# A ring of ten quarters for gathered rows, and VectorE's work placed anew between the links of a chain, in a graph-attention layer

## The chip, the cores and the metric

The kernel runs on one core of one Trainium2 chip. The metric is the device time of one execution in microseconds (us), the median of three timed runs. A further execution was taken with the hardware profiler; its rows are what is read here.

## The reference

One layer of a graph transformer over 3125 nodes of 256 channels, with 50,000 edges sorted by target node. Normalised rows give q, k and v; every edge has a score for each of 8 heads; a softmax over the edges of one target weighs the v rows. A linear attention over all nodes and a mixture of 8 experts stand beside and behind it.

```python
xn = _layernorm(x, axis=-1)
q = xn @ Wq.T + bq; k = xn @ Wk.T + bk; v = xn @ Wv.T + bv
sim = einsum('hed,hed->eh', q[:, dst], k[:, src]) * scale
m = segment_max(sim, dst); p = exp(sim - m[dst]); s = segment_sum(p, dst)
agg = segment_sum((p / s[dst]) * v[src], dst)
x = x + agg @ Wo.T + bo + linear_attention(xn)
x = x + experts(_layernorm(x))
```

## The kernel before

The program runs in stages, each a block of its own that all engines enter together: projections and edge tables (to about 150 us), linear attention (to 204 us), the graph attention (204 to 908.5 us), `finish` (output projection, second norm, routing, to about 970 us) and the experts.

**The graph attention** goes over the edges in 28 chunks (`CH`) of 16 steps of 128 edges; the last chunk has 8 steps. A step is one gather: an indirect DMA that GpSimd issues and that brings 128 rows of k and v (520 floats each, `KV`) from DRAM. Four steps are a quarter (`q` in the code). For chunk n the engines do this:

- GpSimd: per step one index copy and one gather (`gather`, L965, copy L955). Chunk c lies in `slot0` or `slot1` by its parity, four quarters each. Ahead of quarter q of chunk c GpSimd waits until VectorE's `weigh` of the same quarter of chunk c - 2 is done (`pv_made`, `QUADS * c + u // 4 + 1 - 2 * QUADS`).
- TensorE: `spread_q` (L1197) copies the q rows of the targets to the edges; `sums` (L1207) adds the weighted v rows by target, in two pairs of steps per quarter.
- VectorE: `product` (L1058) and `reduce` (L1065) make the scores of a quarter; `weigh` (L1074) multiplies the gathered v by the weights; `add` (L1088) adds a pair's sum to `agg`; `turned_hots` (L1052) makes the table of one-hots for the next `spread_q`.
- ScalarE: `hots` (L992, L996) makes the one-hots for `sums`, here through a buffer `habs`.

**The chain.** The running maxima of a chunk c go through links on several engines: `turn_scores` (TensorE, L1214), `local_maxima` (VectorE, L1100 and L1102), `ends` (TensorE, L1218, L1219), the copy to `row` (ScalarE, L1027), `carries` (VectorE, L1106 to L1111), `columns` (TensorE L1224, then VectorE L1115), `maxima` (VectorE, L1119 to L1123), the exponential (ScalarE, L1035), `turn_weights` (TensorE, L1230), and then `weigh(c, 0)`.

**What sets the order.** Each engine's order is written out by hand in a `body(n, ...)`, called for n = 0 to 29. In round n VectorE makes the scores of chunk n, runs the chain of chunk c = n - 1 and weighs and adds the rest of chunk b = n - 2. Engines run their own order and meet at semaphores. A round is named here by its `local_maxima`. Twelve passes of a hardware loop of two rounds each cover chunks 2 to 25.

`weigh` of (c, 0) and (c, 1) stands late in round c + 1, `weigh` of (c, 2) at the start of round c + 2, and `weigh` of (c, 3) behind that round's `carries`. `m.base` (125 x 25 x 256, the residual) is touched again only in `finish`, and `woT` too.

## Time and profile before

| | us |
|---|---|
| median of 3 timed runs | 1229.21 |
| lowest and highest | 1227.22, 1231.34 |
| the profiled execution | 1221.9 |
| its span (first to last instruction) | 1220.2 |
| graph attention within it | 204 to 908.5 |

The profiled execution is 7.3 us shorter than the median of the timed ones. Of the graph attention, 25 rounds from the second `local_maxima` at 246.95 us to the twenty-seventh at 875.87 us are alike and take 628.92 us, 25.16 us each. Rounds are read here by the wait that an engine ends last on, not by the share of busy time.

### The profile page before, as it was taken

To read this page: it belongs to the slowest core of one execution; us is meant where nothing else is said; L and a number is where in the kernel's file an instruction comes from. 1 tells how busy PE (TensorE), PEld (TensorE's weight loads), DVE (VectorE), ACT (ScalarE), POOL (GpSimd) and SP (SyncE) were. 2 spreads that over 40 slices of the span, in tenths; PEclk is the share of its full clock that TensorE was granted. 3 is DMA by queue.
4 is the path that set the end of the run, shared out by engine and by line. 5 is a ranking of instruction groups with operands and counts; after the bars stand their busy time and mean duration, and the time that the engine had idled before them with its cause. 6 is when DMAs were issued, how large, how long until landed. Compare 5 with 4: busy or idle time off the path is not lost. (4 is left out here: it accounts for less than half of the span.)

```text
span 1220.2 us, 18503 instructions
## 1 busy us (share of the span) xinstructions
PE 940.9 (77%) x4059; PEld 648.3 (53%) x4060; DVE 867.9 (71%) x1761; ACT 478.9 (39%) x1312; POOL 681.8 (56%) x1043
## 2 busy tenths in 40 slices
PE   4899776676777677787777768776768389999996
PEld 3455453454545455555555545554546246666664
DVE  3778767778888788887888788887968604444333
ACT  3556535434444344533444334443433033222330
POOL 2534276567778777787778877887500212222321
PEclk9999877878889877887788878888889779999998
DMA  4344272366566655566556655555413143233310
GB/s 146 103 103 95 79 225 77 89 175 191 164 175 184 179 166 164 170 175 179 153 169 163 173 153 163 154 158 161 116 46 109 63 142 124 90 111 102 137 59 8
DMA packets 79290, 164.39 MB, mean 135 GB/s; under 512 B 15472, under 2 KB 46963, under 8 KB 79251
## 3 DMA queue, kind: packets, MB, share of 16 engines
q0 software_dynamic: 38464, 110.26, 32.7%
q1 hardware_dynamic: 38883, 52.22, 13.3%
q10 hardware_dynamic: 1904, 1.45, 0.4%
q8 instruction: 16, 0.26, 0.1%
q14 instruction: 23, 0.19, 0.1%
HBM read 162.03 MB, written 17.65 MB: 147 GB/s over the span
## 5 line engine op out<-in xcount | busy, mean ns | idle before, releaser
L965 POOL DMA_INDIRECT slot<-kv_d,idx x408 | 426.6, 1046 | 149.3 <-DVE at_pv L1074 87.5
L1207 PE MATMUL at_pa<-at_pv,at_hot 128*125 128x264 f32 x880 | 288.5, 472 | 135.4 <-DVE agg L1088 133.3
L1207 PEld LDWEIGHTS at_pa<-at_pv,at_hot 128*125 128x125 f32 x880 | 186.7, 229 | 214.1 <-DVE agg L1088 140.2
L1197 PE MATMUL at_pq<-q,at_hotT 125*128 x1320 | 190.0, 306 | 11.1 <-POOL at_sign L951 7.0
L1058 DVE TENSOR_TENSOR at_prod<-at_pq,slot 128x1024 f32<-128x1024 f32 x110 | 134.0, 1218 | 76.6 <-DMA slot<-kv_d,idx 72.0
L1197 PEld LDWEIGHTS at_pq<-q,at_hotT 125*128 125x128 bf16 x1320 | 138.8, 109 | 46.0 <-issue 13.9
L1074 DVE TENSOR_TENSOR at_pv<-slot,at_pp 128x1056 f32<-128x1056 f32 x110 | 136.9, 1244 | 15.0 <-PE at_pp L1230 14.8
L992 ACT ACTIVATE at_habs<-iota_w,nloc_e 128x125 f32<-128x125 f32 x440 | 138.0, 384 | 3.4
L1065 DVE TENSOR_REDUCE at_sc<-at_prod 128x32 f32<-128x1024 f32 x110 | 133.4, 1213 | 2.0
L996 ACT ACTIVATE at_hot<-at_habs,one_col 128x500 f32<-128x500 f32 x110 | 78.3, 712 | 126.0 <-PE at_pa L1207 122.6
L1613 POOL DMA_INDIRECT out<-slot,node_s x32 | 31.9, 997 | 166.9 <-DVE slot L1645 166.0
L1680 PE MATMUL xp<-slot,hm 128*128 128x256 f32 (+1 forms) x512 | 113.1, 379 | 0.0
L1634 DVE TENSOR_TENSOR y<-xp,b 128x256 f32<-128x256 f32 (+1 forms) x32 | 13.6, 424 | 139.3 <-PE xp L1680 139.3
L1670 PE MATMUL xp<-hT,slot 128*128 128x489 f32 x256 | 108.6, 583 | 0.8 <-ACT hT L1578 0.8
L1680 PEld LDWEIGHTS xp<-slot,hm 128*128 128x128 f32 (+1 forms) x512 | 94.3, 185 | 18.2 <-issue 3.5
L1088 DVE TENSOR_TENSOR agg<-agg,at_pa 125x264 f32 x220 | 92.6, 421 | 7.6 <-PE at_pa L1207 2.8
L1027 ACT ACTIVATE at_row<-at_pchain 1x256 f32<-1x256 f32 x28 | 10.5, 376 | 202.9 <-PE at_pchain L1219 202.9
L1589 ACT ACTIVATE hm<-xp,b 128x489 f32<-128x489 f32 x64 | 42.9, 671 | 114.5 <-PE xp L1670 114.5
L955 POOL COPY idx<-src_e 128x1 int32 (+1 forms) x408 | 80.5, 198 | 2.6
L1670 PEld LDWEIGHTS xp<-hT,slot 128*128 128x128 f32 x256 | 49.5, 194 | 55.7 <-issue 49.9
L1224 PE MATMUL at_pchain<-at_one_c,at_line 1*128 1x1 f32 x112 | 25.0, 323 | 45.5 <-DVE at_line L1109 45.5
L629 PE MATMUL pa<-slot,xnT 128*125 128x512 f32 x100 | 51.7, 642 | 4.1 <-DVE vst L436 4.1
(316 smaller groups left out, 1263.7 us busy)
## 6 DMA issues: line engine op xcount, KB each, us to landing
slot<-in_w SPq DMA_DIRECT2D x16, 1024.0 KB, 6.3
locrow<-loc_d SPq DMA_DIRECT2D x28, 500.0 KB
slot<-kv_d,idx POOLq DMA_INDIRECT x408, 3.8
kv_d<-vst SPq DMA_DIRECT2D x25, 128.9 KB
base<-in_x SPq DMA_DIRECT2D x5, 625.0 KB
kv_d<-kst SPq DMA_DIRECT2D x25, 125.0 KB
row_d<-base SPq DMA_DIRECT2D x5, 625.0 KB
out<-base SPq DMA_DIRECT2D x1, 3125.0 KB
```

Source lines behind the costliest of these rows:

```text
L955: pool.tensor_copy(m.idx[:, par, u:u + 1], at(m.src_e, c)[:, u:u + 1]).then_inc(S.idx_ready, 1)
L965: pool.indirect_dma_start(slot[par][:, u, :], None, m.kv_d, bass.IndirectOffsetOnAxis(ap=m.idx[:, par, u:u + 1].bitcast(U32), axis=0), bou ...
L992: last = act.activation(habs[:, u % 4, :], m.iota_w[:, :], ACT.Abs, bias=at(m.nloc_e, c)[:, u:u + 1])
L996: act.activation(hot[:, 4 * (g % 2):4 * (g % 2) + 4, :], habs[:, :, :], ACT.Relu, bias=m.one_col[:, 0:1], scale=-1.0).then_inc(S.hot_made, 1)
L1058: dve.tensor_tensor(prod[:, q % 2, :, :], pq[q % 2].rearrange("p (i d) -> p i d", i=4), slot[par][:, 4 * q:4 * q + 4, 0:D], ALU.mult).then ...
L1065: dve.tensor_reduce(sc[:, :, 4 * q:4 * q + 4].rearrange("p h i -> p i h"), prod[:, q % 2, :, :].rearrange("p i (h d) -> p i h d", h=H), X, ...
L1074: dve.tensor_tensor(pv[:, 4 * (q % 2):4 * (q % 2) + 4, :, :], slot[par][:, four, D:KV].rearrange("p i (h c) -> p i h c", h=H), spread(ph[: ...
L1088: dve.tensor_tensor(dst, dst, pa[p % 2][:, 0:H * VW].rearrange("p (h c) -> p h c", h=H), ALU.add).then_inc(S.added, 1)
L1197: mm = pe.matmul(pq[q % 2][:, u * D:(u + 1) * D], hotT[:, 4 * q + u, :], at(m.q3, wins[u // 2])[:, part, :], start=(part == 0), stop=(part ...
L1207: mm = pe.matmul(pa[p % 2][:, 0:H * VW], hot[:, u % 8, :], pv[:, u % 8, :, :].rearrange("p h c -> p (h c)"), start=(u % 2 == 0), stop=(u % ...
L1670: mm = pe.matmul(p1[f % 2][:, 0:CAP], w1[par][:, c, f * 128:(f + 1) * 128], hT[par][:, c, 0:CAP], start=(c == 0), stop=(c == 1))
L1680: mm = pe.matmul(p2[i % 2][0:sizes[i], 0:D], hm[:, f, 128 * i:128 * i + sizes[i]], w2[par][:, f, :], start=(f == 0), stop=(f == FC - 1))
```

## The change

- **Ring.** Gathered rows lie in ten quarters instead of two slots of four: the eight of `slot0` and `slot1`, and two more. Number eight lies where the first 8 tiles (`SOON`) of `m.base` are (with 32 floats more per partition), number nine in a new `m.extra` that also holds `woT`. GpSimd waits ahead of a quarter for the `weigh` of the quarter ten back.
- **Spill.** At the start of the graph attention SyncE stores those 8 tiles (1000 KB) and `woT` (264 KB) to DRAM, ahead of its first load of `locrow`; behind the last `weigh` it loads both back. GpSimd's first two quarters of chunk 2 wait for the store. TensorE's first output projection in `finish`, and VectorE's first addition to `base`, wait for the load.
- **Room.** `prod` has one buffer instead of two; `habs` is gone: `hots` writes `hot` directly, and waits for `summed` ahead of its first instruction; some small tiles of other stages move into `extra`.
- **Loop.** Four passes of five rounds, with three rounds ahead and seven behind, in place of twelve passes of two.
- **Order.** VectorE: `weigh(b, 3)` and `add(b, 2, 0)` stand ahead of `carries`; `product` and `reduce` of quarter 1 stand between `carries` and `columns`; `product` and `reduce` of quarter 2 and `turned_hots` stand between `maxima` and `weigh(c, 0)`. TensorE: `turn_scores` stands ahead of `spread_q(n, 1)`, `ends` ahead of `sums(b, 2)`, `spread_q(n, 2)` ahead of `columns`, `spread_q(n, 3)` ahead of `turn_weights`, and `spread_q(n + 1, 0)` ahead of `sums(c, 0)`.

VectorE in a round near the end, before, from the first scan of the chain to `weigh(c, 0)` (the rows between `fall` and the maxima are `weigh(b, 3)` and the adds of quarter 2):

```order
L1065 TENSOR_REDUCE at_sc<-at_prod 128x4x8 [waits sc_turned,prod_made]
L1106 SCALAR_TENSOR_TENSOR at_run<-at_stop,at_row 1x144 [waits chain_act]
L1107 SCALAR_TENSOR_TENSOR at_run<-at_stop,at_row 1x144
L1109 COPY at_line<-at_run 1x256 [waits chain]
L1110 COPY at_row<-at_run 1x8
L1111 TENSOR_TENSOR at_fall<-at_run 1x8
L1074 TENSOR_TENSOR at_pv<-slot,at_pp 128x1056 [waits summed]
L931 TENSOR_LOAD win_of
L1088 ISA [waits added,summed]
L1088 TENSOR_TENSOR agg<-agg,at_pa 125x264
L1115 COPY at_col<-at_pchain 128x2 [waits chain_pe]
```

Only the reduction covers the first link and only one `weigh` with one `add` the second. The same place now:

```order
L1088 TENSOR_REDUCE at_sc<-at_prod 128x4x8 [waits sc_turned,prod_made]
L1097 TENSOR_TENSOR at_pv<-slot,at_pp 128x1056 [waits summed]
L940 TENSOR_LOAD win_of
L1111 ISA [waits added,summed]
L1111 TENSOR_TENSOR agg<-agg,at_pa 125x264
L1129 SCALAR_TENSOR_TENSOR at_run<-at_stop,at_row 1x144 [waits chain_act]
L1130 SCALAR_TENSOR_TENSOR at_run<-at_stop,at_row 1x144
L1132 COPY at_line<-at_run 1x256 [waits chain]
L1133 COPY at_row<-at_run 1x8
L1134 TENSOR_TENSOR at_fall<-at_run 1x8
L1081 TENSOR_TENSOR at_prod<-at_pq,slot 128x1024 [waits reduced,q_spread,arrived7]
```

The `weigh` and its `add` (L1111) moved ahead of the scans of `carries`, and a `product` took their place behind.

TensorE at the same place, before:

```order
L1214 MATMUL at_pchain<-ident,at_sc 128x128 [waits rescaled,reduced]
L1207 MATMUL at_pa0<-at_pv,at_hot 125x264 [waits pv_made,hot_made,added]
L1207 MATMUL at_pa0<-at_pv,at_hot 125x264
L1207 MATMUL at_pa1<-at_pv,at_hot 125x264 [waits pv_made,hot_made,added]
L1207 MATMUL at_pa1<-at_pv,at_hot 125x264
L1218 MATMUL at_pchain<-ident,at_fwd_max 1x128 [waits chain]
L1219 MATMUL at_pchain<-ident,at_back_max 1x128
L1224 MATMUL at_pchain<-at_one_c,at_line 128x1 [waits chain]
```

And now, behind `spread_q(n, 1)`:

```order
L1243 MATMUL at_pchain<-ident,at_fwd_max 1x128 [waits chain]
L1244 MATMUL at_pchain<-ident,at_back_max 1x128
L1232 MATMUL at_pa0<-at_pv,at_hot 125x264 [waits pv_made,hot_made,added]
L1232 MATMUL at_pa0<-at_pv,at_hot 125x264
L1232 MATMUL at_pa1<-at_pv,at_hot 125x264 [waits pv_made,hot_made,added]
L1232 MATMUL at_pa1<-at_pv,at_hot 125x264
L1222 ISA [waits prod_made]
```

The four matmuls of `sums(b, 2)` went behind the two of `ends`, and `spread_q(n, 2)` (L1222) went ahead of `columns`.

The diff, cut to its core:

```diff
+RING, LOOP, TURN = 10, 3, 5
+LOOPS = (CH - LOOP - 5) // TURN
+SPILL = 32
...
-        prod = sb("prod", [128, 2, 4, D])
+        prod = sb("prod", [128, 4, D])
...
-        habs = sb("habs", [128, 4, TT])
...
         def rounds(eng, body):
-            body(0, 0, 0)
-            body(1, 1, 0)
-            with eng.Fori(1, CH // 2 - 1) as k:
-                body(2 * k, 0, k)
-                body(2 * k + 1, 1, k)
-            for n in range(CH - 2, CH + 2):
-                body(n, n % 2, n // 2)
+            for n in range(LOOP):
+                body(n, n, 0)
+            with eng.Fori(0, LOOPS) as k:
+                for s in range(LOOP, LOOP + TURN):
+                    body(TURN * k + s, s, k)
+            for n in range(CH - 5, CH + 2):
+                body(n, n, 0)
+
+        def place(s, q):
+            return (QUADS * s + q) % RING
...
             @block.sync
             def _(sp):
+                sp.dma_start(m.first_rows..., m.base[:, 0:SOON, :]).then_inc(S.spilled, 16)
+                sp.dma_start(m.wo_d..., m.woT[:, :, :]).then_inc(S.spilled, 16)
...
                 rounds(sp, body)
+                sp.wait_ge(S.pv_made, QUADS * (CH - 1) + quads(CH - 1))
+                sp.dma_start(m.woT[:, :, :], m.wo_d...).then_inc(S.reloaded, 16)
+                sp.dma_start(m.base[:, 0:SOON, :], m.first_rows...).then_inc(S.reloaded, 16)
...
-                            pool.wait_ge(S.pv_made, QUADS * c + u // 4 + 1 - 2 * QUADS)
+                            if s == 2 and q < 2:
+                                pool.wait_ge(S.spilled, 32)
+                            else:
+                                pool.wait_ge(S.pv_made, QUADS * c + q + 1 - RING)
                             pool.nop(nofuse=True)
-                        pool.indirect_dma_start(slot[par][:, u, :], None, m.kv_d,
+                        pool.indirect_dma_start(m.quads[r][:, i, :], None, m.kv_d,
...
                 def hots(c, g):
-                    wait(act, S.hot_made, QUADS * c + g)
+                    four = slice(4 * (g % 2), 4 * (g % 2) + 4)
+                    wait(act, S.summed, PC * c + 2 * g - 2)
...
                 def product(n, s, k, q):
...
-                    wait(dve, S.reduced, QUADS * n + q - 1)
+                    wait(dve, S.reduced, QUADS * n + q)
...
                     if exists(n, 0):
                         reduce(n, 0)
-                    if exists(c):
-                        carries(c)
-
                     if exists(b, 3):
-                        weigh(b, par, 3)
+                        weigh(b, s - 2, 3)
                     if exists(b, 2):
                         wins = windows(b, 2)
                         add(b, 2, 0, wins)
                     if exists(c):
-                        columns(c)
+                        carries(c)
+
+                    if exists(n, 1):
+                        product(n, s, k, 1)
                     if exists(b, 2):
                         add(b, 2, 1, wins)
+                    if exists(n, 1):
+                        reduce(n, 1)
                     if exists(c):
+                        columns(c)
                         maxima(c)
...
+                    if exists(n) and exists(n + 1):
+                        turned_hots(n + 1)
+
+                    if exists(c, 0):
+                        weigh(c, s - 1, 0)
...
+                pe.wait_ge(S.reloaded, 32)
                 for t in range(NT):
```

## Rows read from the trace of the kernel before

**Rows 1.** The page: busy time by engine, and GpSimd's busy tenths in 40 slices

```profile
PE 940.9 (77%) x4059; PEld 648.3 (53%) x4060; DVE 867.9 (71%) x1761; ACT 478.9 (39%) x1312; POOL 681.8 (56%) x1043
POOL 2534276567778777787778877887500212222321
```

**Rows 2.** Busy us by stretch: PE, PEld, DVE, ACT, POOL, clock, DMA share, GB/s

```profile
246.95:875.87 628.92, 466.20 (x2248) 334.88 (x2249) 523.59 (x827) 257.25 (x725) 491.98 (x787) 0.83 0.60 168
```

**Rows 3.** Waits from 247 to 876 us: total, times, longest

```profile
DVE at_prod L1058 <- DMA slot<-kv_d,idx: 66.4, 24, 4.9
DVE at_run L1106 <- ACT at_row L1027: 15.4, 16, 1.3
DVE at_pv L1074 <- PE at_pp L1230: 14.1, 15, 1.5
POOL slot L965 <- DVE at_pv L1074: 73.7, 61, 4.9
```

**Rows 4.** VectorE alone in a stretch of one round: length, busy, clock, DMA share

```profile
272.04:293.33 21.29, 20.85 (x33) 0.92 0.71 196
```

**Rows 5.** Timeline around the one-hot table: start, length, engine, line, idle before

```profile
286.86 1.24 DVE L1074 TENSOR_TENSOR at_pv<-slot,at_pp 128x1056 f32<-128x1056 f32 x1
...
288.02 0.42 DVE L1088 TENSOR_TENSOR agg<-agg,at_pa 125x264 f32 x1
...
288.36 0.74 DVE L1052 TENSOR_SCALAR at_hotT<-locrow,iota_p 125x2048 bf16<-125x2048 bf16 x1
...
288.63 1.37 POOL L965 DMA_INDIRECT slot<-kv_d,idx  x1 [0.15 <-issue]
...
290.35 1.02 POOL L965 DMA_INDIRECT slot<-kv_d,idx  x1 [0.15 <-issue]
```

**Rows 6.** Timeline of GpSimd: ahead of the first gather, first, last gather

```profile
216.38 1.48 POOL L955 COPY idx<-src_e 128x1 int32<-128x1 int32 x8
231.64 1.08 POOL L965 DMA_INDIRECT slot<-kv_d,idx  x1 [13.78 <-DVE at_pv L1074]
...
874.43 1.00 POOL L965 DMA_INDIRECT slot<-kv_d,idx  x1 [0.30 <-issue]
```

**Rows 7.** Gathers of line L965, from issue to landing

```profile
DMA to landing us min/median/max: 2.1/3.8/7.1
```

**Rows 8.** Timeline of VectorE: chunk 2's first product, second and twenty-seventh local maxima

```profile
245.47 1.22 DVE L1058 TENSOR_TENSOR at_prod<-at_pq,slot 128x1024 f32<-128x1024 f32 x1 [5.57 <-DMA slot<-kv_d,idx]
...
246.95 0.41 DVE L1100 TENSOR_TENSOR_SCAN at_fwd_max<-edge,at_pchain 128x128 f32<-128x128 f32 x1
...
875.87 0.41 DVE L1100 TENSOR_TENSOR_SCAN at_fwd_max<-edge,at_pchain 128x128 f32<-128x128 bf16 x1
```

**Rows 9.** TensorE's timeline in one round, low clock, then high; last a window's row

```profile
426.36 2.12 PE L1207 MATMUL at_pa<-at_pv,at_hot 128*125 128x264 f32 x4 [4.62 <-DVE agg L1088]
...
430.52 1.01 PE L1224 MATMUL at_pchain<-at_one_c,at_line 1*128 1x1 f32 x4 [1.61 <-DVE at_line L1109]
431.46 2.74 PE L1197 MATMUL at_pq<-q,at_hotT 125*128 x12
...
437.16 1.48 PE L1197 MATMUL at_pq<-q,at_hotT 125*128 x12
...
467.55 2.02 PE L1207 MATMUL at_pa<-at_pv,at_hot 128*125 128x264 f32 x8 [2.00 <-DVE agg L1088]
...
426.30:435.50 9.20, 7.53 (x26) 5.38 (x27) 7.62 (x18) 4.01 (x13) 5.73 (x11) 0.50 0.51 142
```

**Rows 10.** Last weigh, first output projection, first `locrow` load; an issue row of 1 MB

```profile
903.47 1.25 DVE L1074 TENSOR_TENSOR at_pv<-slot,at_pp 128x1056 f32<-128x1056 f32 x1
...
911.51 2.12 PE L1488 MATMUL opo<-woT,anT 128*125 128x264 f32 x4
...
204.96 0.26 SPq L941 DMA_DIRECT2D locrow<-loc_d  x1
...
slot<-in_w SPq DMA_DIRECT2D x16, 1024.0 KB, 6.3
```

More of the change, by code:

```diff
@@ L977, in _ @@
-                gather(CH - 2, 0, U)
-                gather(CH - 1, 1, U - REST)
+                    index(2, 2, u)
+                gather(2, 2, U)
+                with pool.Fori(0, LOOPS) as k:
+                    for s in range(LOOP, LOOP + TURN):
+                        gather(TURN * k + s, s, U)
+                for c in range(CH - 5, CH - 1):
+                    gather(c, c, U)
+                gather(CH - 1, CH - 1, U - REST)
             @block.scalar
@@ L1173, in body @@
                     if exists(c, 1):
-                        weigh(c, 1 - par, 1)
+                        weigh(c, s - 1, 1)
                     if exists(c, 0):
                         add(c, 0, 0, wins)
-                    if exists(n) and exists(n + 1):
-                        turned_hots(n + 1)
+                    if exists(n, 3):
+                        product(n, s, k, 3)
                     if exists(c, 0):
@@ L1270, in body @@
                         wins = windows(n + 1, 0)
+                    if exists(c):
+                        turn_weights(c)
+                        factor(c)
+                    if exists(n) and exists(n + 1):
+                        spread_q(n + 1, 0, wins)
                     if exists(c, 0):
@@ L1275, in body @@
                         sums(c, 1)
-                    if exists(n) and exists(n + 1):
-                        spread_q(n + 1, 0, wins)
                 pe.wait_ge(S.at_const, AT_CONST)
@@ L1524, in experts @@
         hb = m.hb
[L1525 removed]
+        hT = [m.extra[:, i * 1024:(i + 1) * 1024].rearrange("p (c n) -> p c n", c=2) for i in range(2)]
         hm = sb("hm", [128, FC, 512])
```

114 lines of the change are left out of this document (58 added, 56 removed).

## The prediction, as it was put on record

> **What bounds the kernel now.** I read the page first: in the graph attention no engine is full, and GpSimd (POOL) shows 7 to 8 tenths slice after slice [rows 1]. A table by stretch over 25 like rounds gives VectorE (DVE) 523.59 us busy of 628.92, the most of any engine: a round of 25.16 us with 20.94 us of VectorE work [rows 2]. The waits say what fills the rest: 66.4 us in which VectorE stands at a `product` for gathered rows, in 24 of 25 rounds, 15.4 us at `carries` for ScalarE's row and 14.1 us at `weigh(c, 0)` for the transposed weights [rows 3]. GpSimd, which issues those gathers, waits 73.7 us itself in the same stretch, and for VectorE's `weigh` [rows 3]. That is a circle: a gather waits for a slot that a late `weigh` frees, then the landing takes 2.1 to 7.1 us [rows 7], and VectorE's next `product`, and with it the next `weigh`, comes late by as much. Neither engine is the bound; the two slots are.
>
> Two floors stand under the round. VectorE without any wait: (628.92 - 66.4 - 15.4 - 14.1) / 25 = 21.32 us [rows 2, 3]; one measured stretch from a first `product` to behind the first `add` of the next round holds 21.29 us with 20.85 busy [rows 4]. GpSimd without waits: from the first gather at 231.64 to the end of the last at 875.43 are 643.8 us, less 73.7 of waits, over 408 gathers: 1.397 us each, 22.36 us for the 16 of a round [rows 3, 6].
>
> **The ring.** It lets a gather wait for the `weigh` ten quarters back instead of eight. The worst case before was quarter 2 of a chunk, freed only at the start of the round that uses it. Now the same quarter waits for `weigh(c - 2, 0)`, some 13 us into the round ahead, and is used some 9 us into its own: 18 us apart at a round of 22. Needed are the issue of four gathers (5.6 us) and a landing (3.8, at worst 7.1) [rows 6, 7], 9.4 to 12.7 us. The other three quarters have more. So the 66.4 us go: 2.66 us a round. What is late next is either VectorE's own run with its two link waits, (562.5 / 25 =) 22.50 us, or the gather stream at 22.36. The stream gets a start: GpSimd is free at 217.9 instead of 231.64 [rows 6], and issues two quarters before the first `weigh` is due. That `weigh(0, 0)` now stands behind one more product, reduction and table, about 3 us, so the other 400 gathers start near 234; at 1.397 us each they end near 793, 82 us before the old end. Spread over the rounds that allows 21.9 us a round, so the stream binds only a VectorE that is faster than that.
>
> **A collision that stays.** A gather that begins 0.27 us behind the one-hot table takes 1.37 us where the next takes 1.02 [rows 5]: 0.35 us, once a round, and it is inside the 1.397. The Trainium skill (SBUF — State Buffer, Who interferes with whom) says that a VectorE instruction in a 2-port mode and GpSimd lock one shared port pair, and that the second one waits until the first is done. The row agrees in kind, but shows 0.35 us of a table of 0.74. By the rule alone a busy GpSimd would lose up to 0.74 us a round, the stream would allow 22.3 us and not 21.9, and only the fastest case below would move.
>
> **The order on VectorE.** Two link waits, 15.4 + 14.1 us or 1.18 us a round [rows 3], get more cover. Behind the local maxima stood one reduction, 1.2 us; now a `weigh` (1.16 from start to start) and an `add` (0.34) [rows 5] stand there too. Behind `carries` stood a `weigh` and an `add`, 1.5 us; now a product, an add and a reduction, 2.7 us. Ahead of `weigh(c, 0)` stood a product and a reduction; now also a table and two adds. The work itself is the same, and `reduce` follows its `product` so closely on one in-order engine that the single `prod` buffer costs nothing. The price is on TensorE: `sums(b, 2)` stands behind `ends`, and `columns` behind `spread_q(n, 2)`, where before TensorE did those sums while it waited for the maxima.
>
> I walk one round from the end of the local maxima, at either clock. High (2.4 GHz): `ends` done at 0.4, the first pair of sums at 1.6, VectorE at `add(b, 2, 0)` at 2.3, no wait; both pairs (2.02) and the spread (1.48) [rows 9] end at 4.0, `columns` near 4.6, VectorE there at 6.5, no wait. Low (1.2 GHz): first pair (2.12) [rows 9] done at 2.8, wait 0.5; second pair, spread (2.74) and `columns` (1.01) [rows 9] end near 8.5, VectorE there at 7.0, wait 1.5; then `sums(b, 3)` behind it makes the adds of quarter 3 wait 0.9. So a round costs 21.3 to 21.8 us at the high clock and 21.32 + 2.9 = 24.2 at the low one. The mean clock is 0.83 [rows 2], so 0.17 / 0.5 = 34% of the time, some 8.6 us a round, is at the low level; a stretch of it begins behind an idle TensorE (4.62 us ahead of 426.36, then 9.2 us at 0.50) [rows 9]. That idle time was mostly the gather wait, which goes, but the new order has two pauses of its own, each near 2 us (for the maxima, and for the table). I take low stretches in somewhat under half the rounds, 1.3 us on the mean: **22.6 us a round**, close to the 22.50 that the old order would run without gather waits. 25 x (25.16 - 22.6) = 64 us gained.
>
> ScalarE loses `habs`: all of a quarter's one-hots now wait for the sums two quarters back, not the last step alone. ScalarE has room, 257.25 us busy of 628.92 [rows 2], and one quarter's sums (2.02 us) [rows 9] stand between that wait and the use. I put 0 on it, and as the bound from the nearest row one pair of sums at the high clock, 1 us a round, if that cover is missing.
>
> **Head and tail.** Chunk 2's first product waited 5.57 us [rows 8] for gathers from 231.64; now they start near 218, if the spill is in. Its 1264 KB are issued near 204 and a 1 MB load takes 6.3 us [rows 10], so it lands near 213: no wait. The first load of `locrow` (204.96) [rows 10] queues behind it; it has 11 us until its table, of which the spill takes 7 to 8: 0 to 3 us, I take 1. Net gain 4.6 us. At the end the reload follows the last `weigh` (904.7) and takes 6.3 to 9 us, while the first output projection started at 911.51 [rows 10]: 0 to 5 us, I take 2.5. Loop passes: 4 in place of 12 with longer code; the old rounds show no step from pass to pass, so 0, with 5 us of either sign for code that is loaded more or less often.
>
> **Sum:** 64 + 4.6 - 2.5 = 66 us. The profiled execution of 1221.9 us becomes 1156; it stands 7.3 us below the timed median of 1229.2, so the median becomes **1163 us**.
>
> **Rivals.**
> 1. *The chain is fully covered* and the gather stream binds: 21.9 us a round, 81.5 + 4.6 - 2.5 = 84 us, 1146 (by the skill's rule above 22.3 us and 1156). For it: one stretch already runs without a wait at 21.29 [rows 4]. Against: its clock was high (0.92). Chance 0.12.
> 2. *TensorE's new order meets the low clock in every round:* 24.2 us, 24 + 4.6 - 2.5 = 26 us, 1203; half way it is 1180 to 1195. For it: the mean clock of 0.83 over all 25 rounds, and the two new pauses. Against: the longest pause goes. Chance 0.20.
> 3. *The ring does nothing,* since landing, not the slot, sets the product's start: with 7.1 us for all landings and 3 us of later `weigh(c, 0)` the 18 us above still hold, so rows would have to show slower gathers than any here. 1225 to 1233. Chance 0.03.
> 4. *Slower: TensorE becomes the bound through its clock.* At the high clock its round is 4 x 1.40 for spreads, 4 x 2.02 for sums and about 2.3 for links, 16.0 us, plus 3.5 us of pauses that the new order forces; each us at the low level adds half. Break-even is a round of 25.16 + 2.1 / 25 = 25.24, so 2 x (25.24 - 19.5) = 11.5 us at the low level, against 8.6 now. At 14 us a round is 26.5, and the time 1229 + 33.5 - 2.1 = 1260. Chance 0.04.
>
> The forecast itself, 22.2 to 23.2 us a round, gives 1153 to 1178 and has 0.61. The range of 1148 to 1198 leaves out most of 1, the end of 2, and all of 3 and 4, under 2 in 10. About 0.3% (3.7 us) is what a measurement can tell from no change: faster 0.94, within it 0.02, slower 0.04.
>
> **What the profile after would show.** Right: rounds of 22.2 to 23.2 us between local maxima; under 15 us of waits for gathers in all; first gather near 218; TensorE's clock above 0.85 in the attention; waits of VectorE at adds and `columns` in some rounds only. Wrong: gather waits above 40 us (the ring is not long enough), a clock at or under 0.83 with waits at adds and `columns` of 2 us and more a round (rival 2), or an output projection that waits over 5 us for the reload.

## The result, and the profile after

The changed kernel takes 1186.57 us (median of four runs, 1180.20 to 1187.35) where the kernel before takes 1228.22 (1226.45 to 1231.34): a ratio of 0.9658, 95% interval 0.9613 to 0.9704. A fifth run on record, outside the median, took 1192.17. The change makes the kernel 42 us faster. Forecast were 66 us and a time of 1163, with a range of 1148 to 1198. The profiled execution is the fastest of the four, 1180.2 us with a span of 1178.5.

First the page, as [rows 1]: busy time by engine, and GpSimd's busy tenths in 40 slices.

```profile
PE 915.7 (78%) x4059; PEld 639.7 (54%) x4060; DVE 866.3 (74%) x1761; ACT 484.4 (41%) x1312; POOL 680.0 (58%) x1043
POOL 2533376788888788878887888886000403223321
```

The work is the same, and GpSimd now shows 8 tenths where it showed 7. The 25 like rounds, again from the second to the twenty-seventh `local_maxima`, take 586.30 us or 23.45 each, where [rows 2] had 25.16. The columns are those of [rows 2].

```profile
242.26:828.56 586.30, 443.17 (x2250) 327.02 (x2250) 521.08 (x826) 262.21 (x725) 487.10 (x781) 0.86 0.66 179
```

Then the waits of VectorE (first three rows) and of GpSimd (last two) in the same stretch, which answer to [rows 3].

```profile
DVE agg L1111 <- PE at_pa L1232: 33.0, 33, 2.1
DVE agg L1111 <- issue: 18.5, 23, 2.1
DVE at_pv L1097 <- issue: 9.6, 3, 4.8
...
POOL base L986 <- DVE at_pv L1097: 10.6, 3, 3.9
...
POOL slot L986 <- DVE at_pv L1097: 8.1, 6, 1.9
```

No row on gathered rows is left: the 66.4 us are gone, and so are the waits of `carries` (15.4) and of `weigh(c, 0)` (14.1). Instead VectorE waits 51.5 us at `add` (L1111) and 9.6 us at three `weigh`. GpSimd waits 18.7 us for `weigh` instead of 73.7.

**Which add.** All the gaps ahead of VectorE's instructions in these rounds, summed by their place in the round, come to 61.5 us: 32.8 at `add(c, 0, 0)` (19 rounds), 15.2 at `add(b, 3, 0)` (all 25), 9.6 at the `weigh` that opens a body (3), 3.0 at `add(b, 2, 0)` (10) and 1.0 elsewhere. VectorE's timeline in one round, from the end of `maxima`, shows the three large ones (start, length, engine, line; in brackets the idle time before and what ended it).

```profile
366.09 0.29 DVE L1146 TENSOR_TENSOR at_back_max<-at_pchain,at_back_max 128x128 f32<-128x128 f32 x1
367.02 0.43 DVE L1111 TENSOR_TENSOR agg<-agg,at_pa 125x264 f32 x1 [0.65 <-issue]
...
369.97 0.92 DVE L1075 TENSOR_SCALAR at_hotT<-locrow,iota_p 125x2048 bf16<-125x2048 bf16 x1
370.81 1.23 DVE L1097 TENSOR_TENSOR at_pv<-slot,at_pp 128x1056 f32<-128x1056 f32 x1
...
372.31 1.24 DVE L1097 TENSOR_TENSOR at_pv<-slot,at_pp 128x1056 f32<-128x1056 f32 x1
375.67 0.43 DVE L1111 TENSOR_TENSOR agg<-agg,at_pa 125x264 f32 x1 [2.12 <-PE at_pa L1232]
...
381.20 1.25 DVE L1097 TENSOR_TENSOR at_pv<-slot,at_pp 128x1056 f32<-128x1056 f32 x1 [2.44 <-issue]
```

TensorE in the same time:

```profile
367.53 0.38 PE L1260 MATMUL at_pchain<-at_fall,at_pair 2*125 2x8 f32 x2
371.13 2.74 PE L1222 MATMUL at_pq<-q,at_hotT 125*128 x12 [3.23 <-DVE at_hotT L1075]
373.67 5.17 PE L1232 MATMUL at_pa<-at_pv,at_hot 128*125 128x264 f32 x16
```

TensorE idles 3.23 us for the one-hot table. It comes back at the low clock (a spread takes 2.74 us, where the high clock has 1.48 [rows 9]; the mean granted clock from 371.1 to 378.9 is 0.65), and only behind that spread come the sums for `add(c, 0, 0)`. VectorE stands 2.12 us there. The two pauses of TensorE that the order makes, over the 25 rounds (the table first, then the local maxima):

```profile
PE at_pq L1222 <- DVE at_hotT L1075: 79.3, 25, 3.7
PE at_pchain L1243 <- DVE at_back_max L1125: 57.6, 25, 6.4
```

**Head and tail.** The first gather starts at 216.21 (before 231.64), and the second `local_maxima` at 242.26 instead of 246.95. The reload at the end is late: SyncE's issue, then TensorE's first output projection.

```profile
856.90 0.32 SPq L957 DMA_DIRECT2D base<-first_rows_d  x1
869.32 2.12 PE L1515 MATMUL opo<-extra,anT 128*125 128x264 f32 x4 [6.85 <-DMA base<-first_rows_d]
```

The whole account, profile against profile: before the graph attention -1.6 us, its head -3.1, the 25 rounds -42.6, the last rounds -0.9, from the last `weigh` to the first output projection +6.1 (8.04 to 14.1), the rest +0.5. Together 41.7 us off a span of 1220.2.

### The profile page after: what moved, and what is told of

Read it like the earlier page. It is cut to its first block and busy times, and to the rows that moved or that the text cites. A ratio compares the mean times of both kernels' runs of the same rounds, so it can differ in the third digit from the quotient of the medians.

```text
span 1178.5 us, 17876 instructions
## 1 busy us (share of the span) xinstructions
PE 915.7 (78%) x4059; PEld 639.7 (54%) x4060; DVE 866.3 (74%) x1761; ACT 484.4 (41%) x1312; POOL 680.0 (58%) x1043
## 5 line engine op out<-in xcount | busy, mean ns | idle before, releaser
L986 POOL DMA_INDIRECT slot<-kv_d,idx x320 | 328.9, 1028 | 68.7 <-issue 45.7
L1232 PE MATMUL at_pa<-at_pv,at_hot 128*125 128x264 f32 x880 | 273.2, 465 | 6.3 <-DVE at_pv L1097 4.0
L1222 PE MATMUL at_pq<-q,at_hotT 125*128 x1320 | 190.3, 301 | 95.2 <-DVE at_hotT L1075 83.2
L1016 ACT ACTIVATE at_hot<-iota_w,nloc_e 128x125 f32<-128x125 f32 x440 | 139.0, 387 | 225.7 <-PE at_pa L1232 214.7
L1232 PEld LDWEIGHTS at_pa<-at_pv,at_hot 128*125 128x125 f32 x880 | 191.0, 229 | 61.5 <-DVE agg L1111 14.2
L1222 PEld LDWEIGHTS at_pq<-q,at_hotT 125*128 125x128 bf16 x1320 | 137.5, 107 | 136.4 <-issue 103.3
L1111 DVE TENSOR_TENSOR agg<-agg,at_pa 125x264 f32 x220 | 93.0, 423 | 59.1 <-PE at_pa L1232 38.1
L1097 DVE TENSOR_TENSOR at_pv<-slot,at_pp 128x1056 f32<-128x1056 f32 x88 | 109.6, 1245 | 9.6 <-issue 9.6
L1081 DVE TENSOR_TENSOR at_prod<-at_pq,slot 128x1024 f32<-128x1024 f32 x88 | 107.0, 1216 | 7.5 <-PE at_pq L1222 7.2
L1697 PE MATMUL xp<-extra,slot 128*128 128x489 f32 x256 | 108.1, 581 | 0.8 <-ACT extra L1605 0.8
L1019 ACT ACTIVATE at_hot<-at_hot,one_col 128x500 f32<-128x500 f32 x110 | 78.3, 712 | 3.6
L1697 PEld LDWEIGHTS xp<-extra,slot 128*128 128x128 f32 x256 | 49.3, 193 | 55.4 <-issue 49.6
L986 POOL DMA_INDIRECT base<-kv_d,idx x44 | 45.3, 1031 | 18.1 <-DVE at_pv L1097 10.6
L1243 PE MATMUL at_pchain<-ident,at_fwd_max 128*1 128x128 f32 x28 | 8.1, 289 | 61.1 <-DVE at_back_max L1125 61.1
```

Of the source, the lines that this page charges most:

```text
L986: pool.indirect_dma_start(m.quads[r][:, i, :], None, m.kv_d, bass.IndirectOffsetOnAxis(ap=m.idx[:, r, i:i + 1].bitcast(U32), axis=0), boun ...
L1016: last = act.activation(hot[:, u % 8, :], m.iota_w[:, :], ACT.Abs, bias=at(m.nloc_e, c)[:, u:u + 1])
L1019: act.activation(hot[:, four, :], hot[:, four, :], ACT.Relu, bias=m.one_col[:, 0:1], scale=-1.0).then_inc(S.hot_made, 1)
L1081: dve.tensor_tensor(prod[:, :, :], pq[q % 2].rearrange("p (i d) -> p i d", i=4), m.quads[place(s, q)][:, :, 0:D], ALU.mult).then_inc(S.pro ...
L1097: dve.tensor_tensor(pv[:, 4 * (q % 2):4 * (q % 2) + 4, :, :], m.quads[place(s, q)][:, :, D:KV].rearrange("p i (h c) -> p i h c", h=H), spr ...
L1111: dve.tensor_tensor(dst, dst, pa[p % 2][:, 0:H * VW].rearrange("p (h c) -> p h c", h=H), ALU.add).then_inc(S.added, 1)
```

## The experiments

Ratios are to the kernel before on the same chip in the same set (runs taken together), with 95% intervals. "Gaps" in the text are the idle times ahead of VectorE's instructions in the 25 rounds, by place.

| kernel | us | ratio | 25 rounds, us | clock there |
|---|---|---|---|---|
| changed kernel | 1186.6 | 0.966 (0.961 to 0.970) | 586.3 | 0.86 |
| ring_only | 1160.8 | 0.948 (0.943 to 0.952) | 561.6 | 0.91 |
| order_only | 1226.9 | 0.999 (0.996 to 1.002) | 629.8 | 0.86 |
| straight | 1169.3 | 0.955 (0.950 to 0.959) | 563.3 | 0.88 |
| win_early | 1159.5 | 0.944 (0.937 to 0.951) | 567.1 | 0.88 |
| spread_mid_b | 1178.5 | 0.959 (0.955 to 0.964) | 581.7 | 0.86 |
| old_straight_b | 1147.6 | 0.933 (0.930 to 0.936) | 553.5 | 0.91 |

### The two halves of the change apart: ring_only and order_only

ring_only keeps ring, spill and loop, and has the bodies of VectorE and TensorE in the order of before. order_only has the new order, and its gathers wait as before:

```diff
-                            else:
-                                pool.wait_ge(S.pv_made, QUADS * c + q + 1 - RING)
+                            pool.wait_ge(S.pv_made, QUADS * c + q + 1 - 2 * QUADS)
```

> The changed kernel with its ring, spill and loop, but with VectorE's and TensorE's order of the kernel before. The changed kernel's rounds take 23.45 us, without any wait for gathers, 33.0 us of waits at adds for TensorE's sums and 79.3 us in which TensorE stands for the one-hot table. Theory: the ring alone takes the gather waits, and the new order gives its gain back through that pause of TensorE. Then this kernel has under 5 us of gather waits, its two link waits (carries, weights) of 25 to 35 us come back, the table wait of TensorE falls under 10 us, rounds are 22.5 to 23.2 us and the time is 1170 to 1186, no slower than the changed kernel. Rival: the new order is worth its cover, and without it the link waits grow to 2 us a round, rounds are 23.8 us and more and the time is 1195 to 1205.

> The changed kernel with its order, spill and loop, but a gather waits for the weigh eight quarters back, as two slots would. Theory: the slots were the bound of the kernel before, so gather waits come back with 50 to 90 us (weigh of quarter 0 stands later now), rounds are 24.5 to 25.5 us and the time is 1212 to 1240. Rival: the new order alone did most, gather waits stay under 25 us and the time is under 1200.

The waits of VectorE in ring_only (total, times, longest):

```profile
DVE at_pv L1097 <- issue: 17.0, 3, 6.8
DVE at_run L1129 <- ACT at_row L1050: 8.7, 12, 1.7
...
DVE at_pv L1097 <- PE at_pp L1253: 1.3, 1, 1.3
```

The row of its 25 rounds:

```profile
242.75:804.37 561.62, 425.94 (x2248) 309.26 (x2249) 522.18 (x826) 263.20 (x725) 488.38 (x778) 0.91 0.68 188
```

And the two largest waits of VectorE in the rounds of order_only:

```profile
DVE at_prod L1080 <- DMA slot<-kv_d,idx: 34.7, 19, 3.9
DVE agg L1110 <- PE at_pa L1231: 32.7, 45, 2.1
```

ring_only shows no gather wait, as its theory says, but its link waits came to 10.0 us and not to 25 to 35, and its time lies 9 us under the theory's range. order_only lies in the range of its theory, with somewhat fewer gather waits than the 50 us given (44.9).

The ring (with its spill and loop) is worth 66 us, and the new order takes some 25 of them back, 24.7 in the rounds. With the ring and the old order the wait of `weigh(c, 0)` falls by itself, from 14.1 to 1.3 us, and that of `carries` from 15.4 to 8.7. Without the ring the new order hides the link waits and a third of the gather waits (44.9 us are left of 66.4), and pays for it at the adds (49 us) and at the loop ends (7.9). It is worth nothing (0.999).

**Why the link waits fell.** The wait at `carries` goes with TensorE's clock just ahead of it. In the kernel before it is 1.05 to 1.30 us in the nine rounds whose last 2.5 us ahead of `carries` have a clock of 0.50 or 0.51, and 0.12 us in the nine at 0.98 to 1.00. One round of the first kind, then the windows (2.5 us up to `carries`) of this round and of the next, which is of the second kind (columns as in [rows 2]):

```profile
250.08 0.45 DVE L1106 TENSOR_TENSOR_SCAN at_run<-at_stop,at_row 1x144 f32<-1x144 bf16 x1 [1.29 <-ACT at_row L1027]
...
247.58:250.08 2.50, 2.05 (x6) 0.91 (x4) 1.21 (x3) 0.41 (x2) 0.82 (x2) 0.50 0.76 213
272.97:275.47 2.50, 1.37 (x6) 0.83 (x6) 2.38 (x5) 0.41 (x2) 2.17 (x5) 1.00 0.86 268
```

In ring_only 22 rounds have a clock of 1.00 there and wait 0.12 to 0.46 us. The other three wait 1.38 to 1.75 us, at 0.61 to 0.66, and they are the three behind a loop end, where VectorE had stood for 4.9 to 6.8 us. So a long stop of VectorE lets TensorE idle and its clock fall, and the next link is late by it: most of what the new order was to cover at `carries` was an echo of the gather waits. For `weigh(c, 0)` only the totals speak for the same, so that is not shown.

### Where the new order pays: win_early, spread_mid

win_early moves one step on VectorE: the load of the two window numbers of quarter 3 into registers, which stood between `maxima` and `add(b, 3, 0)`.

```diff
                     if exists(b, 2):
                         add(b, 2, 1, wins)
+                    if exists(b, 3):
+                        wins = windows(b, 3)
                     if exists(n, 1):
                         reduce(n, 1)
...
                     if exists(b, 3):
-                        wins = windows(b, 3)
                         add(b, 3, 0, wins)
```

> The changed kernel with one register load of VectorE (the windows of quarter 3) moved from behind the maxima to ahead of the second reduction. In the changed kernel the add behind it waits 0.47 to 0.65 us in each of 25 rounds, 15.3 us in all. Theory: the load cannot start until the short maxima have been issued and its length is in the open there; behind a long instruction it is covered. Then that wait is gone in every round and the time falls 8 to 15 us, to 1172 to 1179, less what the later wait at the add of quarter 0 takes back. Rival: the add waits for TensorE's sums of quarter 3, then the wait stays, and the time is 1184 to 1188.

The place of that gap in VectorE's timeline of win_early:

```profile
338.50 0.29 DVE L1146 TENSOR_TENSOR at_back_max<-at_pchain,at_back_max 128x128 f32<-128x128 f32 x1
338.78 0.43 DVE L1111 TENSOR_TENSOR agg<-agg,at_pa 125x264 f32 x1
```

In the changed kernel 0.93 us lie between the starts of these two, here 0.28. The theory holds: the 15.2 us are gone in all 25 rounds. `add(c, 0, 0)` falls from 32.8 to 26.0 us, and the loop ends cost 15.4 instead of 9.6. The rounds are 19.2 us shorter. The medians differ by 27 us, more than either theory said, and more than the rounds show; the profiled executions (spans of 1178.5 and 1158.4) differ by 20. So 19 to 20 us are read from the traces, and the rest is not explained.

The cause of such a gap is in the code: `windows` fills registers, and the `add` needs them for its address, so it can't start before they are there. Behind a long instruction the load is hidden; behind the last one of `maxima` (0.29 us) it shows 0.47 to 0.65 us. The load itself in the changed kernel (shortest, median and longest in ns):

```profile
L940 DVEq TENSOR_LOAD <-win_of x110: 524/529/780, 230.5 to 857.4; - x110
```

The Trainium skill (DMA: Bandwidth & Descriptors, Latency and other measured facts) gives a floor of about 600 ns for `tensor_load`; the median here is 0.53 us, somewhat below it.

spread_mid changes TensorE alone:

```diff
-                    if exists(n) and exists(n + 1):
-                        spread_q(n + 1, 0, wins)
                     if exists(c, 0):
                         sums(c, 0)
+                    if exists(n) and exists(n + 1):
+                        spread_q(n + 1, 0, wins)
                     if exists(c, 1):
```

> In the changed kernel add(c, 0, 0) waits in 19 of 25 rounds, 32.8 us in all, because TensorE first does spread_q(n + 1, 0) (2.74 us at the low clock, behind 3.2 us of idling for the one-hot table) and only then sums(c, 0). Here spread_q(n + 1, 0) stands between sums(c, 0) and sums(c, 1); nothing else is moved. If that order causes the wait: it falls from 32.8 to under 8 us, TensorE no longer idles for the table ahead of the sums, and the kernel is 15 to 28 us faster than the changed one, 1160 to 1172 us. If the wait is only the low clock, and the clock stays as it is, the wait comes back at add(c, 0, 1) or at the first product of the next chunk, and the time stays within 5 us of 1186.6.

That run came out at 1473.05 us beside 1312.73 of the kernel before, in a set that is told of below; so the kernel was run again.

> The kernel of spread_mid again, since on the chip of that run TensorE's results reached ScalarE and VectorE up to 13 us behind its records, with the kernel before at 1312.7 us too. Where the kernel before takes about 1228 us: if the place of spread_q(n + 1, 0) causes the wait of add(c, 0, 0) (32.8 us in the changed kernel), that wait falls under 8 us and the time is 1160 to 1172 us; if it is the low clock alone, the wait comes back at add(c, 0, 1) or the next chunk's first product, and the time is 1181 to 1192 us.

1178.52 us: neither theory. The wait at `add(c, 0, 0)` fell to 19.0 us, but it is in every round now, 0.76 us each, and small ones came behind it (6.0 us at `add(c, 0, 1)`, 4.3 at the `add` behind the `weigh` that opens a body). The largest wait of VectorE and of TensorE in its rounds:

```profile
DVE agg L1111 <- PE at_pa L1232: 26.5, 52, 0.8
...
PE at_pa L1232 <- DVE at_pv L1097: 113.4, 25, 4.8
```

So the spread ahead of the sums explains the 2 us waits (the longest is 0.83 us now), not all of them. What remains is, by the order in the code, VectorE's own: between `weigh(c, 0)`, which the sums need, and `add(c, 0, 0)` stands one further `weigh` and a rescale, 1.5 us, and TensorE, which has idled 4.5 us for that `weigh`, is not back in time. The old order has a product and a reduction there as well, and ring_only shows no wait at this `add`. No run moved them alone.

### The loop ends: straight

straight is the changed kernel with all rounds written out, GpSimd's loop too (the diff is cut):

```diff
-            for n in range(LOOP):
-                body(n, n, 0)
-            with eng.Fori(0, LOOPS) as k:
-                for s in range(LOOP, LOOP + TURN):
-                    body(TURN * k + s, s, k)
-            for n in range(CH - 5, CH + 2):
+            for n in range(CH + 2):
                 body(n, n, 0)
```

> The changed kernel with all its rounds written out, no hardware loop in the graph attention. The three rounds in which the changed kernel goes back to the loop's start take 26.59, 26.57 and 25.50 us, the others 23.1 on the mean, and there VectorE, TensorE and ScalarE stand without a releaser for up to 4.8 us. Theory: a taken branch to code 5 rounds back costs some 3 us a time. Then no round is over 24.5 us, and the time is 7 to 10 us under that of the changed kernel, 1176 to 1180. Rival: the long code costs wherever it is new, not at the branch, so the written-out kernel is no faster, 1184 to 1192, with stalls spread over rounds.

It is 17 us faster (23 in the rounds; 6 of them were lost ahead of the graph attention, where nothing was changed). No round is over 23.7 us, so the theory holds, but the gain is twice what it gave. The gaps fell by 21 us: 9.6 at the loop ends, 3.3 at the register loads (11.9 us instead of 15.2), 5.7 at `add(c, 0, 0)` and 2.2 at `add(b, 2, 0)`. How large a loop end can be is plain in ring_only, on VectorE:

```profile
369.77 1.22 DVE L1088 TENSOR_REDUCE at_sc<-at_prod 128x32 f32<-128x1024 f32 x1
376.33 1.26 DVE L1097 TENSOR_TENSOR at_pv<-slot,at_pp 128x1056 f32<-128x1056 f32 x1 [5.34 <-issue]
```

The `weigh` is the first instruction of a body behind the jump back, and nothing in the profile releases it ("issue"). Three such gaps make 17.0 us in ring_only, 15.4 in win_early, 9.6 in the changed kernel, none in straight. The queue that loads instructions (packets, MB, share) moved more too. Its row on the page after:

```profile
q14 instruction: 80, 0.65, 0.2%
```

And on the page before:

```profile
q14 instruction: 23, 0.19, 0.1%
```

And its row within the gap above (371.0 to 376.3), then within the first of the changed kernel (378.8 to 381.2):

```profile
q14 instruction: 2, 0.02, 0.9%
...
q14 instruction: 2, 0.02, 1.7%
```

Two or three such packets of 8 KB fall into each loop-end gap of these kernels. straight loads much code too (28 packets on this queue in its 25 rounds, where the changed kernel has 59 and the kernel before 3) and shows no gap. So it is the jump back that costs, not the length of the code.

The Trainium skill (Runtime: NRT & Kernel Launch, Instruction fetch mechanics) says that an engine holds two lines of 16 KiB of its instructions, fetches ahead only in sequence, and stalls for a fetch when it jumps to code outside them. The rows agree: a pass of two rounds (before) shows no gap at its end, one of five rounds shows 2.4 to 6.8 us. From what length of a pass on it stalls, no run shows.

### The reload: reload16

```diff
-                sp.dma_start(m.base[:, 0:SOON, :], m.first_rows.rearrange("p (t d) -> p t d", t=SOON)).then_inc(S.reloaded, 16)
+                for a, z in ((0, 112), (112, TT)):
+                    sp.dma_start(m.base[a:z, 0:SOON, :], m.first_rows[a:z, :].rearrange("p (t d) -> p t d", t=SOON)).then_inc(S.reloaded, 16)
```

> The changed kernel, with the load of the eight residual tiles behind the last weigh given as two DMAs of 112 and 13 partitions instead of one of 125. In the changed kernel that load took 12.4 us, and the first output projection waited 6.85 us for it. If the shape of 125 partitions is what makes it slow (the 1 MB loads of 128 partitions took 6.3 us): landing in 6 to 8 us, the first output projection waits under 1.5 us, the kernel 5 to 7 us faster, 1180 to 1182 us. If it is the direction or the row length: 12 us again, and no change.

The time of this run says nothing on it (1429.9 us beside 1312.7 of the kernel before, see below), but the transfer can be read in the timeline: its issue by SyncE, and the first output projection on TensorE.

```profile
1113.52 0.86 SPq L958 DMA_DIRECT2D base<-first_rows_d  x2
...
1120.66 1.13 PE L1516 MATMUL opo<-extra,anT 128*125 128x264 f32 x4 [0.23 <-ACT anT L1486]
```

TensorE starts 7.1 us behind the issue and waits for ScalarE's `anT`, not for the load. The kernel warm, on the same chip and with the single DMA of 125 partitions, waits 7.31 us for it. In old_straight_b, which has the split as well, 7.2 us lie between issue (824.52) and output projection (831.73). The share of the 16 DMA engines that is busy tells why. Two windows within the reload (columns as in [rows 2]), of the changed kernel and of old_straight_b:

```profile
858.90:860.90 2.00, 0.07 (x1) 0.00 (x0) 1.40 (x4) 0.00 (x0) 1.00 (x7) 1.00 0.30 127
...
826.50:828.50 2.00, 0.04 (x1) 0.00 (x0) 1.43 (x4) 0.00 (x0) 1.04 (x8) 1.00 1.02 340
```

A share of 0.30 is 5 engines of 16; with the split all are busy. The next stage's load of weights is issued 3.8 us behind the reload in both kernels, so it doesn't make the difference. So the number of partitions made the 12.4 us. The Trainium skill (DMA: Bandwidth & Descriptors, Why a DMA increments its semaphore by 16 and not by 1) has the rule: a DMA runs on the largest number of engines up to 16 that divides its slowest dimension, which is 5 for 125 and 16 for 112. The shares of 0.30 and 1.02 agree.

### The best of both: old_straight

Ring, old order, rounds written out, reload split.

> The ring with the old order of VectorE and TensorE, no hardware loop (every round written out), and the load of the residual tiles in two DMAs. The kernel with ring and old order took 1160.8 us, with three stalls of 5.3, 6.8 and 4.9 us at its loop ends and a round of 21.7 us elsewhere. Theory A (VectorE binds, loop ends cost what they show): 17 us for the stalls and 6 for the reload go, 1137 to 1141 us, gather waits of VectorE under 5 us. Theory B (then the gather stream binds, 1.40 us for each of 400 gathers from 233 us, so that the last one ends near 793 us): VectorE waits 5 to 15 us for gathered rows in all, GpSimd waits for nothing, the rounds go no lower than 21.9 us, 1143 to 1150 us.

This run took 1271.92 us beside 1312.73 of the kernel before (0.969, 0.962 to 0.976), in the same disturbed set, and so the kernel was run again.

> The kernel of old_straight again, for the same reason. Theory A (VectorE binds, the loop ends cost what they show in the kernel with ring and old order): 1137 to 1141 us where the kernel before takes about 1228, gather waits of VectorE under 5 us. Theory B (the gather stream binds): VectorE waits 5 to 15 us for gathered rows, GpSimd waits for nothing, rounds of 21.9 us and more, 1143 to 1150 us.

1147.57 us, ratio 0.933: 83 us faster than the kernel before in its set, and 39 less than the changed one took in another. VectorE's waits in its rounds:

```profile
DVE at_prod L1074 <- DMA slot<-kv_d,idx: 8.8, 2, 4.5
DVE at_run L1122 <- ACT at_row L1043: 7.2, 12, 1.3
```

The time and the gather waits are those of theory B, but its mechanism holds in part only. Most rounds take 21.6 us, under its floor of 21.9. GpSimd, whose gathers start 1.38 us apart (22.1 us for 16), loses half a microsecond a round against that, and waits 0.9 us in all for `weigh`. Chunk 2's first `product` finds the last gather of its quarter issued 19.6 us ahead, chunk 14's only 3.7 us. There, and again at chunk 21, VectorE stands 4.5 and 4.2 us for a gather. The first of the two in its timeline, then SyncE's load of the next `locrow`, and the time from issue to landing of the gather that it waits for (issued at 494.41):

```profile
502.70 1.23 DVE L1074 TENSOR_TENSOR at_prod<-at_pq,slot 128x1024 f32<-128x1024 f32 x1 [4.54 <-DMA slot<-kv_d,idx]
...
493.95 0.25 SPq L948 DMA_DIRECT2D locrow<-loc_d  x1
...
DMA to landing us min/median/max: 8.3/8.3/8.3
```

A landing in the usual 3.8 us would have cost VectorE 0.1 us or nothing. Each time the late gather was issued just behind a load of `locrow` (500 KB), and this is the rule: of the 357 gathers in these rounds whose landing the trace has, the 48 issued up to 1 us ahead of such a load or up to 2 us behind it land in 6.2 us (median), the others in 3.8. So both are needed, a head start that GpSimd has used up and a slow landing. The first rival of the prediction, the gather stream as the bound, comes next once order and loop ends are out of the way, and the load of `locrow` decides what it costs.

### Two sets in which TensorE's results came late: warm, warm_b, old_direct

In two sets the kernel before took 1312.7 and 1317.2 us, not 1227 to 1230: warm, reload16, spread_mid and old_straight in one, warm_b and old_direct in the other. The second of them ran on the chip on which ring_only and the kernels of its set ran undisturbed. The kernels of a set are compared only with one another. warm puts idle matmuls into TensorE's pause for the table:

```diff
+                    if exists(c) and exists(n) and exists(n + 1):
+                        wait(pe, S.prod_made, QUADS * (n + 1) - 1)
+                        for i in range(WARM):
+                            pe.matmul(pq[0][:, 0:128], m.ident[:, :], m.ident[:, :], start=True, stop=True)
                     if exists(n) and exists(n + 1):
                         spread_q(n + 1, 0, wins)
```

> Tests the clock alone. The order stays that of the changed kernel, but TensorE does eight matmuls of 128x128 on the identity, whose result nothing reads, in its pause for the one-hot table ahead of spread_q(n + 1, 0). If the clock falls because of that pause: the granted clock rises from 0.86 to above 0.92 in the rounds, add(c, 0, 0) waits under 1 us a round instead of 1.3, and the kernel is 8 to 20 us faster, 1167 to 1178 us. If the pause for the local maxima (57.6 us in all) or the whole load sets the clock: clock within 0.02 of 0.86, and the time the same or up to 5 us longer, since the idle matmuls delay the spread.

> The kernel of warm again, where TensorE's records and the arrival of its results agree: the order of the changed kernel, with eight matmuls of 128x128 on the identity, whose result nothing reads, in TensorE's pause for the one-hot table. If that pause lets the clock fall: granted clock above 0.92 in the rounds instead of 0.86, add(c, 0, 0) waits under 15 us in 25 rounds instead of 32.8, and 1165 to 1178 us where the changed kernel takes 1186.6. If the pause for the local maxima or the load sets the clock: clock within 0.02 of 0.86, the waits as they were, 1184 to 1192 us. Moving spread_q(n + 1, 0) behind the first sums (spread_mid_b) left 19.0 us of that wait, 0.76 in every round, and gave 1178.5 us.

1416.72 us, and 1418.15 the second time (ratios 1.079 and 1.084). In both, and in reload16 and spread_mid, one wait outweighs the rest. In reload16, the changed order otherwise, TensorE's records have `ends` and both pairs of `sums(b, 2)` by 494.2, and VectorE adds the first pair only at 504.88 (TensorE's row, then VectorE's):

```profile
492.22 2.02 PE L1233 MATMUL at_pa<-at_pv,at_hot 128*125 128x264 f32 x8
...
504.88 0.43 DVE L1112 TENSOR_TENSOR agg<-agg,at_pa 125x264 f32 x1 [10.73 <-remote]
```

"remote" means that the profile has no instruction that released it. Such gaps at `add(b, 2, 0)` make 222 to 225 us in these kernels (25 rounds; 205 in the first run of warm). What holds TensorE's results back there is open: no row shows it, and it was not looked for by a run of its own. The comparison of warm with reload16, in the same set and the same order, does bear on the clock. The gaps at `add(c, 0, 0)` are 26.2 us in reload16 and 10.6 in warm (9.1 in warm_b, in the other set), and the clock in the rounds is 0.76 against 0.80 (0.79). The waits are those of the first theory, under 15 us; the clock stayed far under its 0.92. That speaks for the pause as the cause of most of that wait, but it is not shown for an undisturbed set, and no gain in time was measured.

old_direct takes the index copies out of old_straight: each gather reads its indices from the table itself.

```diff
-                                                bass.IndirectOffsetOnAxis(ap=m.idx[:, r, i:i + 1].bitcast(U32), axis=0),
+                                                bass.IndirectOffsetOnAxis(ap=at(m.src_e, c)[:, u:u + 1].bitcast(U32), axis=0),
```

> The kernel of old_straight_b (ring, old order, rounds written out, reload in two DMAs; 1147.6 us) without the index copies: with the rounds written out, each gather reads its indices straight from the table of sources, so GpSimd issues a gather every 1.17 us (1.02 busy and 0.15 between) instead of every 1.38. If the gather stream bound that kernel (its two gather waits of 4.5 and 4.2 us fell where the stream had used up its start): no gather waits left, rounds of 21.5 us, 1136 to 1142 us; GpSimd waits for weigh instead, 2 to 3 us a round. If VectorE binds it anyway, and those two waits were slow landings: they stay, or come elsewhere, and the time is 1144 to 1150 us.

1372.58 us beside 1317.2 (1.047), worse than old_straight in the other disturbed set (0.969). The rate can be read from GpSimd's timeline: gathers start 1.30 us apart, not 1.17, since 0.30 us lie between them without the copy.

```profile
609.35 0.99 POOL L979 DMA_INDIRECT slot<-kv_d,src_e  x1 [0.30 <-issue]
```

So even at its best this edit gives 0.08 us a gather, 1.3 us a round. VectorE's first product of a chunk waited in every round, up to 8.7 us ("issue"), but not for rows: the last gather of its quarter had been issued 22 to 27 us ahead, and in old_straight_b none took over 8.4 us to land. (This trace has no landing of a gather.) Beside the rows and VectorE's own work a product waits for TensorE's spread alone; so in this set it was the spread that came late. Whether VectorE or the gather stream would bind in an undisturbed set is open.

## Why the prediction was right, and where it was off

The time lies in the range, the ring was read right, and one term failed that the ring's gain outweighs.

**The ring** was read right. All 66.4 us of gather waits went, the first gather came at 216.21 (forecast near 218), and ring_only, which has only the spill and the loop beside the ring, gains the 66 us that the prediction gave to the whole. That is chance in part: in ring_only the rounds take 22.46 us, where 22.50 was forecast for the old order without gather waits, but they are made of 21.7 us in the ordinary rounds and some 5 us more at three loop ends. The link waits fell to 10.0 us when the gather waits went, with the clock. The prediction had kept them whole, at 29.5. These 19.5 us too many and the 17.0 us of loop ends, put at 0, nearly cancel.

**The order on VectorE: this step failed.** It said that the 29.5 us of link waits get more cover and that the price is 0 to 2.9 us a round, in low stretches only; 22.6 us a round came out as 23.45. Against the old order with the ring the new one was to cost 2.5 us in all (22.6 against 22.50 a round); it cost 24.7 (23.45 against 22.46). The walk had the places of its waits wrong:
- `columns` (1.5 us at the low clock): 0 measured, in all rounds.
- `add(b, 2, 0)` (0.5): 3.0 us in 10 rounds, no more than 0.35 each.
- `add(c, 0, 0)` (not in the walk): 32.8 us, the largest. The walk ended at the adds of quarter 3 and took the pause for the table as a matter of the clock. It did not ask what stands behind that pause on TensorE: a spread, and only then the sums that this `add` needs.
- the register load of `windows(b, 3)` (not in the walk): 15.2 us. In the order of before a `weigh` or a product always stood ahead of an `add`; the row of the load is in the order shown, and it was passed over because no row of before had a gap for it.

Together 51 us, 2.0 a round, against the 1.3 that were put on the low clock.

**The clock.** Forecast above 0.85; it is 0.86, against 0.91 for the same ring with the old order. The two pauses that the new order makes are longer than the 2 us given: 57.6 us in all for the maxima and 79.3 for the table, 2.3 and 3.2 a round. Half of rival 2 has come true, with 23.45 us a round between the forecast and its 24.2.

**Loop passes.** Put at 0 with 5 us of either sign, "the old rounds show no step from pass to pass". They are short. Three gaps of 2.4 to 4.8 us cost 9.6 us, beyond the bound of 5; up to 17.0 where no other wait hides them.

**Reload.** Put at 2.5 us of 0 to 5, from a 1 MB load of 128 partitions in 6.3 us [rows 10]. This one has 125 partitions, ran on 5 of the 16 DMA engines (share 0.30) and took 12.4; the step cost 6.1. The first output projection waits 6.85 us, over the 5 that the prediction named as wrong.

**The gather stream.** The prediction took 7.1 us as the worst landing. In old_straight_b gathers beside a load of `locrow` take up to 8.4 us, and two of them cost VectorE 8.8 us. The gather of [rows 5] began 0.27 us behind the start of the one-hot table, so 0.47 us of the table were left, not 0.74, and 0.35 of them showed.

**Spill, ScalarE.** The spill let the first gathers go without a wait, and the head gained 3.1 us of 4.6. ScalarE's one-hots made VectorE wait nowhere, as said.

The sum in the terms of the prediction: 64 + 4.6 - 2.5 = 66 became 42.6 + 3.1 - 6.1 = 40, with 2 us elsewhere. Of the 24 us missing from sum to measurement 21 are in the rounds, and 9.6 of those are the loop ends.

## What to carry to other kernels

Waits at the links of a chain may be an echo of the large wait elsewhere, by way of TensorE's clock: take that one out alone, look again, and only then move instructions. An order that fills one engine's gaps makes pauses on the engine that it waits for, so walk both engines through the whole round, with what stands behind each pause, each register load, and the jump of the loop. A DMA's rate is read from a row with the same number of partitions, not only the same bytes.

## What the runs showed of the hardware

- A jump back over five written-out rounds costs VectorE 2.4 to 6.8 us, with two or three packets of the instruction queue in each gap; over two rounds, nothing that shows.
- A link through TensorE makes VectorE wait 1.05 to 1.30 us at a granted clock of 0.50 and 0.12 at 1.00, in the kernel before.
- A gather of 128 rows issued within 1 us ahead of a 500 KB load of `locrow` or 2 us behind it lands in 6.2 us, any other in 3.8 (medians, old_straight_b).
- 1000 KB as one DMA of 125 partitions took 12.4 us at a DMA share of 0.30; as 112 and 13 partitions, 7.2 us or less at 1.02.
- A load of two numbers into VectorE's registers takes 0.53 us; 0.47 to 0.65 us of idle time show where the instruction ahead is short, and 0.48 at most with constant addresses.
- An indirect gather without an index copy between is followed by 0.30 us of pause, against 0.15 behind a copy: leaving the copy out brings 0.08 us a gather, not 0.21.
- In two of the four sets of experiments TensorE's results reached ScalarE and VectorE up to 13 us behind its recorded matmuls, once a round, and the kernel before took 1313 to 1317 us. There the new order of the change was slower than the kernel before (1.08 to 1.12). Of the two kernels with ring and old order one was faster (0.969) and one, old_direct, slower (1.047).
